# Weight products ahead of the first tile, split into rounded halves, with the splitting given to three engines

## What is computed

```python
# block 1: attention in a window of 34 positions, per batch
score = einsum('nqh,hk,nlk->nql', layernorm(x), W_a, enc)
align = softmax(where(mask, -1e9, score)) * gauss
x = x + tanh(concat([align @ enc, layernorm(x)]) @ W_c.T)
# block 2: routing to 64 slots, a GRU step on the slots, attention among slots
h = gelu(concat([layernorm(x), mean(slots)]) @ w1 + b1)
alpha = softmax of the top 8 of (h @ w2 + b2) / (|tau| + 0.1)
S = GRU(alpha.T @ layernorm(x) / sum(alpha), slots)
y = layernorm(S + attention(S)); out = x + alpha @ (y @ wvp + bvp) @ wo + bo
```

## Time and profile before

| | us |
|---|---|
| median of 3 runs | 354.89 |
| profiled execution, own time | 356.68 |
| its span, first to last instruction | 354.6 |
| TensorE busy | 339.5 (96%) |
| VectorE / GpSimd / ScalarE busy | 257.1 / 212.7 / 189.5 |
| mean granted TensorE clock | 0.995 |
| TensorE enters tile 0 | 42.79 |

### The profile page before, as it was taken

One profiled execution on the slowest core, in us unless ns is written; L12 is line 12 of the kernel. 1 busy time (PEld: TensorE's weight loads), 2 busy tenths in 40 slices (PEclk: granted clock), 3 DMA queues, 4 the chain that ended last, 5 costly groups with the idle time before them and its releaser, 6 DMA issues.

```text
span 354.6 us, 7007 instructions
## 1 busy us (share of the span) xinstructions
PE 339.5 (96%) x2280; PEld 279.1 (79%) x2280; DVE 257.1 (72%) x737; ACT 189.5 (53%) x389; POOL 212.7 (60%) x354
## 2 busy tenths in 40 slices
...
GB/s 277 234 348 397 277 146 195 106 76 118 61 120 60 98 85 90 89 62 111 69 70 110 61 32 2 2 0 167 361 46 2 0 0 1 2 0 0 268 392 291
DMA packets 40934, 42.79 MB, mean 121 GB/s; under 512 B 3245, under 2 KB 32045, under 8 KB 40898
## 3 DMA queue, kind: packets, MB, share of 16 engines
...
q10 hardware_dynamic: 1522, 1.27, 1.1%
q0 software_dynamic: 288, 0.66, 0.7%
...
## 4 chain that ended last, share of the span: by engine, by line
PE 70%; DVE 12%; POOL 6%; issue 6%; ACT 4%; DMA 1%; POOLq 0%; SPq 0%; ACTq 0%; DVEq 0%
PE psum L410 15%; PE psum L411 13%; PE psum L412 13%; PE psum L1588 5%; PE psum L1428 5%; PE psum L1853 3%; PE psum L1616 3%; PE psum L1470 2%; PE psum L1569 2%; POOL X L561 2%; PE psum L1651 1%; DVE st L882 1%; DMA WvpT<-in_WvpT 1%; PE psum L1498 1%; PE psum L1802 1%
## 5 line engine op out<-in xcount | busy, mean ns | idle before, releaser
L410 PE MATMUL psum<-GW_hi,hT_hi 128*128 128x292 f32 (+1 forms) x256 | 78.9, 308 | 1.1 <-POOL GW_lo L543 1.0
L412 PE MATMUL psum<-GW_lo,hT_hi 128*128 128x292 f32 (+1 forms) x256 | 73.9, 289 | 0.0
L411 PE MATMUL psum<-GW_hi,hT_lo 128*128 128x292 f32 (+1 forms) x256 | 73.8, 288 | 0.0
L561 POOL TENSOR_TENSOR X<-X,th 128x512 f32<-128x512 f32 x32 | 38.4, 1199 | 30.3 <-ACT th L1210 30.3
L556 POOL TENSOR_TENSOR hT_lo<-xT,hT_hi 128x512 fp32r<-128x512 f32 x32 | 43.4, 1357 | 12.4 <-ACT hT_hi L1166 12.4
L410 PEld LDWEIGHTS psum<-GW_hi,hT_hi 128*128 128x128 f32 x256 | 48.4, 189 | 3.1 <-issue 2.2
L411 PEld LDWEIGHTS psum<-GW_hi,hT_lo 128*128 128x128 f32 x256 | 48.3, 189 | 0.2 <-issue 0.2
L412 PEld LDWEIGHTS psum<-GW_lo,hT_hi 128*128 128x128 f32 x256 | 48.1, 188 | 0.0
L410 PE MATMUL psum<-xhT_hi,w_hi 128*128 128x256 f32 x128 | 38.4, 300 | 0.1
L411 PE MATMUL psum<-xhT_hi,w_lo 128*128 128x256 f32 x128 | 36.1, 282 | 0.0
L412 PE MATMUL psum<-xhT_lo,w_hi 128*128 128x256 f32 x128 | 36.0, 282 | 0.0
(11 more groups left out here) (292 smaller groups left out, 888.5 us busy)
## 6 DMA issues: line engine op xcount, KB each, us to landing
...
```

What stands on the lines that cost most here:

```text
L410: pe.matmul(out, w_hi, m_hi, start=start, stop=False)
L411: pe.matmul(out, w_lo, m_hi, start=False, stop=False)
L412: return pe.matmul(out, w_hi, m_lo, start=False, stop=stop)
L561: pool.tensor_tensor(tile_x(r), tile_x(r), halves(th[:, :]), ALU.add).then_inc(S("x2"), 1)
```

## The change

The G and EW products, and chunks 2 and 3 of the `Wp` product (`SPLIT_WP`), are made by `mm3` from rounded halves. The halves need new instructions:

- ScalarE makes `Wvp_hi`, `Wo_hi` (two chunks each), `WaT_hi` (this takes the place of the subtraction in place), `Wc1T_hi` (four chunks), and now also `GW_hi` (four) and `EW_hi` (three), which VectorE made before.
- GpSimd makes `Wvp_lo`, `Wo_lo` (two chunks each) ahead of the `Wc2_raw` sums, and `Wc1T_lo` (four chunks) behind them, ahead of `hT_lo`.
- VectorE makes, per chunk, `encWT_hi`, `encWT_lo` and `WaT_lo`, directly behind `encWT`. The seven small steps stand behind those. The wide instructions on `GW` are cut into four.

TensorE's order becomes: nine products of ones, `Wp` chunks 0 to 2, the turned windows, `Wp` chunk 3, G (chunk `k` outside, so that all four banks end in the last chunk), the column mean, the slot mean, EW. `Wc2_raw` is issued ahead of the wait for the gather and `Wc1T` right behind it; `w1b` follows tile 0. The place of the buffers changes with it (`Wc1T_lo` and `encWT_lo` overwrite `Wc1T` and `encWT`).

```diff
-HB_DONE, G_DONE, WM_DONE, EW_DONE = 1, 1, KC + 2, KC + 2
+G_DONE, WM_DONE, HB_DONE, EW_DONE = 0, KC + 1, KC + 2, KC + 2
+HI_WA, HI_WC1, HI_GW, HI_EW = 4, 4 + KC, 4 + 2 * KC, 4 + 3 * KC
+BVZ_DONE, SUM_DONE, LOW_WC1, LOW_WP = 5, 6, 6, 6 + KC
+SPLIT_WP = (2, 3)
...
-WARM = 7
+WARM = 9
...
     WaT = place("WaT", [P, KC, D], F32, "early_x")
+    region("early_x2", cursor["early_x"])
     Wc1T = place("Wc1T", [P, KC, D], F32, "early_x")
+    Wc1T_lo = place("Wc1T_lo", [P, KC, D], F32R, "early_x2")
...
+    WaT_hi = place("WaT_hi", [P, KC, D], F32R, "a3")
+    region("a3", cursor["x"] + KC * (WS + D) * 4)
+    WaT_lo = place("WaT_lo", [P, KC, D], F32R, "a3")
...
+    encWT_lo = place("encWT_lo", [P, KC, NG * WP], F32R, "early3")
...
+        sp.dma_start(Wc2_raw[:, :, :], chunks("WcT", KC)).then_inc(S("in_wc2"), 16)
         sp.wait_ge(S("encw"), 16 * NG)
-        sp.dma_start(w1b[:, :, :], chunks("w1", KC)).then_inc(S("in_w1b"), 16)
-        sp.dma_start(Wc2_raw[:, :, :], chunks("WcT", KC)).then_inc(S("in_wc2"), 16)
+        sp.dma_start(Wc1T[:, :, :], chunks("WcT")).then_inc(S("in_wc1"), 16)
         x_load(0)
         xT_load(0)
-        sp.dma_start(Wc1T[:, :, :], chunks("WcT")).then_inc(S("in_wc1"), 16)
+        sp.dma_start(w1b[:, :, :], chunks("w1", KC)).then_inc(S("in_w1b"), 16)
         for t in range(1, 4):
             x_load(t)
...
+        for n, k in enumerate(SPLIT_WP):
+            pool.wait_ge(S("wa"), 2 * n + 1)
+            pool.tensor_tensor(Wvp_lo[:, n, :], WvpT[:, k, :], Wvp_hi[:, n, :].bitcast(F32), ALU.subtract).then_inc(S("wcs"), 1)
+            pool.wait_ge(S("wa"), 2 * n + 2)
+            pool.tensor_tensor(Wo_lo[:, n, :], Wo[:, k, :], Wo_hi[:, n, :].bitcast(F32), ALU.subtract).then_inc(S("wcs"), 1)
...
+            pool.wait_ge(S("wa"), HI_WC1 + k + 1)
+            pool.tensor_tensor(Wc1T_lo[:, k, :], Wc1T[:, k, :], Wc1T_hi[:, k, :].bitcast(F32), ALU.subtract).then_inc(S("wcs"), 1)
...
+            v.tensor_copy(encWT[:, c, :], banks[c][:, 0:NG * WP]).then_inc(S("encWT"), 1)
+        v.wait_ge(S("encWT"), KC)
+        count["encWT"] = KC
...
+            link(v.tensor_copy(encWT_hi[:, k, :], encWT[:, k, :]), "encWT")
+            count["encWT"] += ENC_PARTS - 1
+            v.tensor_tensor(encWT_lo[:, k, :], encWT[:, k, :], encWT_hi[:, k, :].bitcast(F32), ALU.subtract).then_inc(S("encWT"), 1)
+            v.wait_ge(S("wa"), HI_WA + k + 1)
+            v.scalar_tensor_tensor(WaT_lo[:, k, :], WaT[:, k, :], wneg[:, k:k + 1], WaT_hi[:, k, :].bitcast(F32),
+                                   ALU.add, ALU.subtract).then_inc(S("encWT"), 1)
+        v.tensor_scalar(gw[0:WP, :], gw[0:WP, :], geo[:, 1:2], None, ALU.max).then_inc(S("first_row"), 1)
...
+        stats1(0)
...
+            link(v.tensor_copy(G_hi[:, c, :], src), "g")
+            v.tensor_tensor(G_lo[:, c, :], src, G_hi[:, c, :].bitcast(F32), ALU.subtract).then_inc(S("g_lo"), 1)
+        v.wait_ge(S("pre"), WM_DONE)
+        for k in range(KC):
+            v.tensor_tensor(Wc2_raw[:, k, :], Wc2_raw[:, k, :], banks[7], ALU.add).then_inc(S("split"), 1)
         v.wait_ge(S("pre"), HB_DONE)
-        v.tensor_tensor(hb[:, :], banks[0][:, 0:HC], b1, ALU.add).then_inc(S("first_row"), 1)
+        v.tensor_tensor(hb[:, :], banks[6][:, 0:HC], b1, ALU.add).then_inc(S("first_row"), 1)
+        stats1(1)
...
+            v.wait_ge(S("wa"), HI_GW + k + 1)
+            v.tensor_tensor(GW_lo[:, k, WS:], Wc2_raw[:, k, :], GW_hi[:, k, WS:].bitcast(F32), ALU.subtract).then_inc(S("split"), 1)
...
-        link(v.tensor_tensor(Wc2_raw[:, :, :], Wc2_raw[:, :, :], bc(banks[0], KC, 1), ALU.add), "split")
-        link(v.tensor_copy(GW_hi[:, :, WS:], Wc2_raw[:, :, :]), "split")
-        link(v.tensor_tensor(GW_lo[:, :, WS:], Wc2_raw[:, :, :], GW_hi[:, :, WS:].bitcast(F32), ALU.subtract), "split")
...
+            v.wait_ge(S("wa"), HI_EW + g + 1)
+            v.scalar_tensor_tensor(EW_lo[:, g, :], banks[4 + g][0:WP, :], gw[0:WP, g:g + 1],
+                                   EW_hi[:, g, :].bitcast(F32), ALU.mult, ALU.subtract).then_inc(S("ew"), 1)
...
+            act.wait_ge(S(f"in_wo{k}"), 32)
+            act.copy(Wvp_hi[:, n, :], WvpT[:, k, :]).then_inc(S("wa"), 1)
+            act.copy(Wo_hi[:, n, :], Wo[:, k, :]).then_inc(S("wa"), 1)
...
-            act.activation(WaT[:, c, :], WaT[:, c, :], ACT.Identity, bias=wneg[:, c:c + 1]).then_inc(S("wa"), 1)
+            act.activation(WaT_hi[:, c, :], WaT[:, c, :], ACT.Identity, bias=wneg[:, c:c + 1]).then_inc(S("wa"), 1)
         for c in range(KC):
             act.wait_ge(S("wp_mm"), c + 1)
             act.copy(Wp[:, c, :], banks[4 + c]).then_inc(S("wp"), 1)
+        act.wait_ge(S("in_wc1"), 16)
+        for k in range(KC):
+            act.copy(Wc1T_hi[:, k, :], Wc1T[:, k, :]).then_inc(S("wa"), 1)
...
+            act.wait_ge(S("split"), k + 1)
+            act.copy(GW_hi[:, k, WS:], Wc2_raw[:, k, :]).then_inc(S("wa"), 1)
+        act.wait_ge(S("first_row"), 1)
+        for g in range(NG):
+            act.wait_ge(S("pre"), EW_DONE + g + 1)
+            act.activation(EW_hi[:, g, :], banks[4 + g][0:WP, :], ACT.Identity, scale=gw[0:WP, g:g + 1]).then_inc(S("wa"), 1)
...
+                pe.wait_ge(S("wcs"), 2 * n + 2)
             for c in range(KC):
-                last = pe.matmul(banks[4 + c], WvpT[:, k, c * P:(c + 1) * P], Wo[:, k, :], start=k == 0, stop=k == KC - 1)
+                at_c = slice(c * P, (c + 1) * P)
+                if k in SPLIT_WP:
+                    last = mm3(pe, banks[4 + c], Wvp_hi[:, n, at_c], Wvp_lo[:, n, at_c], Wo_hi[:, n, :], Wo_lo[:, n, :],
+                               False, k == KC - 1)
+                else:
+                    last = pe.matmul(banks[4 + c], WvpT[:, k, at_c], Wo[:, k, :], start=k == 0, stop=False)
                 if k == KC - 1:
                     last.then_inc(S("wp_mm"), 1)
...
+            pe.wait_ge(S("encWT"), KC + ENC_PARTS * (k + 1))
+            for c in range(KC):
+                at_c = slice(c * P, (c + 1) * P)
+                last = mm3(pe, banks[c][:, 0:NB * WS], WaT_hi[:, k, at_c], WaT_lo[:, k, at_c],
+                           encWT_hi[:, k, 0:NB * WS], encWT_lo[:, k, 0:NB * WS], k == 0, k == KC - 1)
+                if k == KC - 1:
+                    last.then_inc(S("pre"), 1)
+        pe.wait_ge(S("wcs"), SUM_DONE)
+        pe.wait_ge(S("wp"), KC)
+        pe.matmul(banks[7], cmean[:, :], wcs[:, :], start=True, stop=True).then_inc(S("pre"), 1)
...
+                pe.wait_ge(S("first_row"), 2)
+            at_g = slice(g * WP, (g + 1) * WP)
+            for k in range(KC):
+                pe.wait_ge(S("wcs"), LOW_WC1 + k + 1)
+                last = mm3(pe, banks[4 + g][0:WP, :], encWT_hi[:, k, at_g], encWT_lo[:, k, at_g],
```

More of the change, by code:

```diff
@@ L169, in program @@
     encw = place("encw", [WP, NG, D], F32, "early")
+    region("early3", cursor["early"])
     encWT = place("encWT", [P, KC, NG * WP], F32, "early")
+    encWT_lo = place("encWT_lo", [P, KC, NG * WP], F32R, "early3")
     w2_raw = place("w2_raw", [P, HC, NS], F32, "early")
@@ L173, in program @@
     region("early2", at_of("h1T"))
+    region("early4", at_of("w1"))
+    Wc1T_hi = place("Wc1T_hi", [P, KC, D], F32R, "early4")
+    assert cursor["early4"] <= at_of("xT")
     region("ewx", at_of("xT") + 4 * KC * P * 4)
```

109 lines of the change are left out of this document (47 added, 62 removed).

## The result

| | before | after |
|---|---|---|
| median of runs | 354.77 us (4 runs, 354.13 to 356.19) | 360.31 us (4 runs, 359.28 to 360.63) |
| profiled execution, its span | 356.68, 354.6 | 360.16, 358.4 |
| tile 0 begins, first turned weights | 42.79, 48.77 | 46.82, 52.17 |
| TensorE, VectorE, GpSimd busy | 339.5, 257.1, 212.7 | 336.2, 268.7, 225.8 |

The changed kernel takes 1.0146 times the time of the kernel before, with a 95% interval of 1.0109 to 1.0182: it is slower by 1.5%, 5.5 us on the medians (forecast: 359.6). Between the two profiled executions lie only 3.5 us. One thing is needed to read this: the 29 runs of the kernel before that stand beside the first four experiments fall into two groups, 14 from 353.8 to 354.9 and 15 from 355.7 to 357.3, and the profiled execution of before, 356.68, lies where the second does.

A forecast was written before the change was run, and what follows sets the result against it. TensorE was taken to bound the preparation before the change, VectorE's chain alternating with GpSimd after it. The cost of 4.7 us added to the median of 354.89 gave 359.6, range 350.0 to 362.5.

The forecast's parts named there:

- turns between VectorE and GpSimd: In G's preparation the engines alternate whole instructions on shared SBUF ports; chunk 3 is ready at 33.4, not 23.2.
- TensorE's saving of 4.8: Cheaper rounded products in the preparation save TensorE 1.3 us in Wp, 1.5 in G and 2.0 in EW.
- Transfers: Loads ahead of G: WaT lands at 14.69 as before, Wc2_raw at 16.6; landing at 15.4 or 18 moves -1 or +1.2.
- VectorE's list of 13.0: VectorE's queued work after chunk 3, from small steps to GW_lo and keys, takes 13.0 us and sets tile 0 at 46.7.
- turn for the keys: At the end of VectorE's queue ahead of tile 0, one wait of 0.6 us for GpSimd at the keys.
- TensorE's own path: From chunk 3 at 33.4 through column mean, slot mean and EW, TensorE reaches 46.0, 0.7 shorter than VectorE's path.
- +4.7: Cost at the end of stack, ahead of the turned weights: 53.4 against 48.71, carried to the kernel's end.
- The reference point: Cost added to the median: 354.89 + 4.7 = 359.6; against the profiled execution, 1.79 above the median, 361.4.
- Rival 1: Faster: VectorE does not stand behind GpSimd in the G chain, TensorE bounds, turned weights at 43.6; 349.7 us, chance 0.21.
- Rival 2: No change: Wc2_raw lands early and two of six turns in the G chain fall away; +1.5, 356.4 us, chance 0.10.
- Rival 3: Slower still: TensorE's clock falls to the lower level in idle stretches; 361.4, up to 362.1 us, chance 0.12.
- the two idle stretches: TensorE waits in G ahead of chunk 2 and again ahead of chunk 3, about 3.4 us each.

The follow-up runs named there:

- the first four experiments: e1, e2, e4 and the changed kernel with both e1's and e2's edits (355.28 us); the kernel before had a median of 355.68 us beside them.
- e1: Changed kernel with one added wait: GpSimd starts Wc1T_lo only after VectorE's last WaT_lo; 354.93 us, ratio 0.9985 to the kernel before.
- e5: Changed kernel with one added wait: GpSimd's second Wc2_raw sum and everything behind it follow VectorE's last WaT_lo; 353.04 us, ratio 0.9933 to the kernel before.
- e9: e5 with the Wp product left whole in full precision; 351.96 us, ratio 0.9918 to the kernel before.
- e10: e9 with the G product in full precision too, so only EW is split; 351.88 us, ratio 0.9924 to the kernel before.
- e12: e10 with EW in full precision too, so no split is left; 354.56 us, ratio 0.9988 to the kernel before.
- e2: Changed kernel with the load of Wc2_raw issued behind the wait for the gather; 360.71 us, ratio 1.0136 to the kernel before.
- e11: e5 with GpSimd's four steps on Wvp and Wo put behind VectorE's window steps; 352.30 us, ratio 0.9924 to the kernel before.
- e4: Kernel before with nine warm-up products instead of seven and nothing else; 355.07 us, ratio 1.0001 to the kernel before.
- e7: Changed kernel with seven warm-up products instead of nine; 360.35 us, ratio 1.0135 to the kernel before.
- e6: Changed kernel with Wp whole, the gather ahead of Wc2_raw, and all GpSimd sums and Wc1T_lo behind the last WaT_lo; 354.30 us, ratio 0.9951.
- e8: Changed kernel with the gather ahead of Wc2_raw, all GpSimd sums and Wc1T_lo behind the last WaT_lo, Wp still split; 354.47 us, ratio 0.9974.

## Why the prediction was right

**The sign and the size.** Forecast 359.6, measured 360.31, 1.0146 times before. The mechanism was the one forecast, turns between VectorE and GpSimd; e1 and e5 show it, since a wait that only keeps GpSimd out of the way gives back 5.4 and 7.3 us (medians, of different batches). Not all of it is turns in the chain: the blocked `stack` (0.7) and, from e1 to e5, the clock in G (1.4) are in it.

**TensorE's saving of 4.8.** Right per instruction, of little use as a sum. The products are as short as said: 0.23 for 512 columns, about 0.13 for 288. But of Wp 1.3, G 1.5 and EW 2.0 only EW's 2.0 reaches tile 0 even where nothing is in the way (e9, e10, e12). Two small slips in the working change nothing: 4 by 0.95 is 3.8, not 3.7, and 60 products by 0.014 are 0.8, not 0.9.

**Transfers.** Here a step was off: I had Wc2_raw landing at 16.6 and everything else as before. It landed at about 18.9. `WaT` was late as well (`junk` starts at 16.20, 14.69 before), which e2 and the other traces do not tie to the load order, and so were the windows, which they do: they were turned at 17.00, behind a wait that the forecast did not have. That Wp still ended at 21.1, as forecast, is luck: the clock rose earlier than assumed (chunk 2 began at 12.3, not 14.5), and the wait took that back. Chunk 0 was ready at 23.7, not 21.8, chunk 1 at 25.1, not 23.2.

**The turns.** 9 turns as counted (three beside chunk 0 to the sums, six in chunks 2 and 3). GpSimd could start on `Wc1T_lo` only at 24.54 (forecast 23.0). From there the six turns took 9.6 us (forecast 10.1), so chunk 3 was ready at 34.1, forecast 33.4.

**Downstream.** VectorE's list of 13.0 took 11.7 (`GW_lo` ends at 45.8) and no turn for the keys fell to it; `brz` and the statistics followed at once, not after tile 0. TensorE's own path, forecast 0.7 shorter, was the later one: EW ended at 46.8 with no idle ahead of tile 0, while the keys were ready at 46.36. It took 12.7 us from chunk 3 on, forecast 12.6. Tile 0: forecast 46.7, measured 46.82. That they agree so well is luck in part, as the chain was 0.7 late and the list that was to set tile 0 was 1.3 short. From there to the end of `stack` it took 5.3, not 6.7, as VectorE's list was already further. So +3.4 at the turned weights where +4.7 was forecast, and +3.5 between the profiled executions. This is the term that was mis-sized.

**The reference point.** I added the cost to the median of 354.89, though the sum was made against an execution that was 1.8 above it. The changed kernel's profiled execution is no higher than its own median. So the medians are 2.0 further apart than the profiled executions, and the two errors, a cost 1.3 too high and a reference point 1.8 too low for it, nearly cancel. That the median is met to within 0.7 us is this luck. The experiments say the same: e5, e9, e10 and e11 are 4.0 to 4.9 below 356.68 in their profiled executions, and 2.4 to 3.2 below before in their medians. Why before's profiled execution lies above its median is open. An early clock at the start is not enough: e4's profiled execution has it and took 355.93. Both have the blocked `stack`, and 0.2 us decides whether it is blocked; whether it is free at 354 us no trace shows.

**The rivals.** Rival 1 (ports free for VectorE) fell, yet its milestone, turned weights at 43.6, was right for the undisturbed case: e5, e9, e10 and e11 have them at 43.65 to 44.07. This is luck in part: tile 0 came at 39.0 to 39.5, not 38.4, and the turned weights 4.6 behind it, not 5.2, and of the three splits counted in it only EW's is needed. Rival 2 (fewer turns) fell. Rival 3 (the clock) happened in the changed kernel for 3 us only, in chunk 2, where it cost nothing that counts. Its sign, weight loads of 0.33 after 28 us, was there all the same, from 29.98 to 32.14, so that sign alone did not tell the rival from the forecast. In e1 and e7 the clock fell in G; in e2, e6 and e8 it fell ahead of EW and stayed down far into it, where, with the pause ahead of it, it cost up to 4 us of tile 0. I had named the two idle stretches as its place, and 2.5, 2.6 and 1.3 us came instead of twice 3.4.
